# Spatial transforms of a spectral block in four 64x64 parts of the matmul array

## The reference, cut to what matters

```python
# layer 0: whitening over all 50,176 tokens
m = mean(x_flat); f = x_flat - m
ff = (1 - EPS) * (f @ f.T / (n - 1)) + EPS * eye(64)
x = (inv(cholesky(ff)) @ f) * gamma + beta
# layer 1: spectral filter, then MLP
residual = x
h = layer_norm(x, n1_g, n1_b)                      # over the 64 channels
xf = rfft2(h, axes=(height, width), norm='ortho')  # 56 x 29 frequencies
o1 = relu(complex product of xf with w1, 8 blocks of 8 channels, + b1)
o2 = softshrink(complex product of o1 with w2 + b2, 0.01)
h = irfft2(o2) + h + residual
out = gelu(layer_norm(h, n2_g, n2_b) @ mw1 + mb1) @ mw2 + mb2 + h
```

## Time and profile before

| | |
|---|---|
| median of three runs | 841.62 us (840.57 to 844.27) |
| profiled execution, device time | 842.9 us |
| its span, first to last instruction | 841.1 us |
| TensorE busy | 778.3 us, 93% |
| VectorE busy | 569.4 us, 68% |
| ScalarE busy | 378.4 us, 45% |
| GpSimd busy | 251.9 us, 30% |
| mean granted clock of TensorE, share of 2.4 GHz | 0.932 |

### The profile page before, as it was taken

The page is one execution under the profiler, slowest core; times in us unless marked ns, Lnnn a source line. Parts: engine busy times, 40 slices in busy tenths (PEclk is TensorE's granted clock), DMA queues, the critical chain, the costliest instruction groups (busy, mean ns, idle before and its releaser), DMA issues.

```text
span 841.1 us, 17115 instructions
## 1 busy us (share of the span) xinstructions
PE 778.3 (93%) x6823; PEld 542.9 (65%) x6823; DVE 569.4 (68%) x1860; ACT 378.4 (45%) x687; POOL 251.9 (30%) x107
## 2 busy tenths in 40 slices
PE   7999996986799999999999999999999998989987
PEld 5985555875477667666766667676757664746433
DVE  4567777279577767776776777677867695843551
ACT  0011005623164735563556455545554545455455
POOL 4000000932903270427042604360435045413000
PEclk9895557899699999999999999999999999999999
DMA  9943002002000121002100300030001001001012
GB/s 263 276 113 107 1 0 75 3 2 78 1 1 13 34 65 46 24 23 82 29 25 23 95 17 24 23 108 4 23 23 34 2 24 34 23 2 34 23 34 67
DMA packets 10369, 39.41 MB, mean 47 GB/s; under 512 B 1282, under 2 KB 1410, under 8 KB 8834
## 3 DMA queue, kind: packets, MB, share of 16 engines
q1 hardware_dynamic: 10290, 38.31, 15.8%
HBM read 25.46 MB, written 12.85 MB: 46 GB/s over the span
## 4 chain that ended last, share of the span: by engine, by line
PE 80%; DVE 15%; issue 3%; ACT 1%; DMA 0%; DVEq 0%; ACTq 0%
PE psum L1069 11%; PE psum L1078 10%; PE psum L982 7%; PE psum L1047 6%; PE psum L992 6%; PE psum L1023 6%; PE psum L1034 6%; PE psum L1007 6%; PE psum L966 5%; PE psum L829 4%; PE psum L886 4%; DVE stats L588 3%; PE psum L1087 3%; PE psum L953 2%; PE psum L1060 2%
## 5 line engine op out<-in xcount | busy, mean ns | idle before, releaser
L1271 ACT ACTIVATE hid<-psum,hbias 128x448 f32<-128x448 f32 x224 | 124.0, 636 | 80.6 <-PE psum L1069 80.6
L436 POOL TENSOR_TENSOR p_y<-layer,clamped 128x512 f32<-128x512 f32 x64 | 75.5, 1180 | 240.1 <-DVE clamped L698 240.1
L1069 PE MATMUL psum<-n2T,mw1s 64*128 64x448 f32 x448 | 102.7, 577 | 1.7 <-ACT n2T L1264 1.7
L1078 PE MATMUL psum<-hid,prm 128*64 128x448 f32 x448 | 96.3, 552 | 2.0 <-DVE oslice L707 2.0
L401 POOL TENSOR_TENSOR hbuf<-hbuf,prm 112x3584 f32<-112x3584 f32 x7 | 43.4, 6205 | 111.1 <-DVE hbuf L653 111.1
L1047 PE MATMUL psum<-u_r,cst 58*112 58x448 f32 x256 | 60.4, 592 | 15.5 <-DVE rbuf L720 11.3
L1023 PEld LDWEIGHTS psum<-w2s,o_g 128*64 128x64 f32 x1856 | 60.1, 138 | 15.5 <-issue 8.9
L692 DVE TENSOR_TENSOR layer<-psum,prm 128x512 f32<-128x512 f32 x64 | 40.4, 631 | 41.6 <-PE psum L1023 41.6
L1034 PEld LDWEIGHTS psum<-cst,p_y 128*128 128x128 f32 x512 | 61.2, 192 | 11.2 <-issue 5.6
L1023 PE MATMUL psum<-w2s,o_g 128*64 128x64 f32 x1856 | 66.3, 224 | 2.1 <-DVE layer L692 2.1
L1034 PE MATMUL psum<-cst,p_y 128*128 128x112 f32 x512 | 66.7, 277 | 1.2 <-DVE layer L692 1.2
(11 more groups left out here) (130 smaller groups left out, 1308.7 us busy)
## 6 DMA issues: line engine op xcount, KB each, us to landing
xin<-x_dram SPq DMA_DIRECT2D x8, 1568.0 KB, 8.3
out_dram<-oslice SPq DMA_DIRECT2D x56, 224.0 KB, 2.2
ybuf<-x_dram SPq DMA_DIRECT2D x2, 1568.0 KB, 16.8
fbuf<-x_dram SPq DMA_DIRECT2D x2, 1568.0 KB, 19.9
xin<-x_dram SPq DMA_DIRECT2D x4, 392.0 KB, 5.2
n<-x_dram SPq DMA_DIRECT2D x1, 1568.0 KB, 22.1
n<-x_dram SPq DMA_DIRECT2D x4, 392.0 KB, 15.7
prm<-params_dram SPq DMA_DIRECT2D x1, 742.0 KB, 3.9
```

What stands on the lines that cost most here:

```text
L436: nc.gpsimd.tensor_tensor(yk, a, b, ALU.subtract).then_inc(y_ready, 1)
L1069: nc.tensor.matmul(t[:, 0:4 * ROWS], mw1s[C * v:C * v + C, HH * m:HH * m + HH], n2T[C * v:C * v + C, s % 2, :], start=True, stop=True).the ...
L1078: last = nc.tensor.matmul(t[C * v:C * v + C, 0:4 * ROWS], pp("mw2")[:, C * m:C * m + C], hid[:, s % 2, m, v, :], start=(m == 0), stop=(m = ...
L1271: nc.scalar.activation(hid[:, s % 2, m, v, :], bank[CH_MLP[i].bank[k]][:, 0:4 * ROWS], ACT.Gelu, bias=hbias[:, m:m + 1]).then_inc(c_act, 1)
```

## The change

- Tiles whose partitions are rows of images have 128 partitions and not 112: image 0 on 0 to 55, image 1 on 64 to 119 (`RP` is 128); only the loads of x still come with 112. Between them lie rows of zeros, which two more memsets (`mlp_t`, `xT`) and columns of zeros in the constants provide.
- `dft_h` and `dft_w` are cut into matmuls on 64x64 parts of the array. In `dft_h` image b is on the part's rows (partition 64 b) and channel half h on its columns; in `dft_w` the halves are on the rows and the images on the columns. `f1` and `f2` shrink to 58 columns. A chunk now has eight groups of 58 columns; two chunks (two banks) are filled together, and both banks are waited for before the first matmul.
- h lies as (channel j, half h, place w). g1 and b1 then repeat along w.
- ScalarE's copies and activations keep their number, except in step 0, where `dft_w` has one activation for a chunk and not two.
- Whitening, the transpositions and the inverse column transform work on 128 partitions or columns where they had 112.
- Two store DMAs for a slice, one for each image.
- VectorE: `ev_mlp` of pair i-2 comes behind all four `ln2_stats`, and `multiply_rstd` of the second half moves from `ln2` to the end of slice 0 (`second_half`), in front of the first statistics of the next pair.

The core of the diff:

```diff
+RP = 128
-CONST_COLS = {"ident": 128, "below": C, "minus": C, "f1": 2 * KR, "f2": 4 * KF, "invw": 112, "invh": 2 * ROWS,
+CONST_COLS = {"ident": 128, "below": C, "minus": C, "f1": KR, "f2": KR, "invw": 112, "invh": 2 * RP,
...
-        u_v = u_r[0:ROWS, :].rearrange("p (m j) -> p m j", j=CH)
+        u_v = u_r[0:C + H, :].rearrange("p (k b s j) -> p k b s j", b=2, s=2, j=CH)
+        xT_v = xT[:].rearrange("p (w b r) -> p w b r", b=2, r=C)[:, :, :, 0:H]
+        mlp_t_v = mlp_t[:].rearrange("p (w b r) -> p w b r", b=2, r=C)[:, :, :, 0:H]
...
-        h_w = h_nat.rearrange("p (j m) -> p j m", j=CH)
-        h_tok = h_nat.rearrange("p (j w h) -> p w j h", j=CH, h=2)
+        h_w = h_nat.rearrange("p (j h w) -> p j h w", j=CH, h=2)
+        h_tok = h_nat.rearrange("p (j h w) -> p w j h", j=CH, h=2)
...
-                    sp.dma_start(o[:, s * SW * C:(s + 1) * SW * C], oslice[:, s % 2, :]).then_inc(stored[s % 2], 16)
+                    for b in range(2):
+                        sp.dma_start(o[H * b:H * b + H, s * SW * C:(s + 1) * SW * C],
+                                     oslice[C * b:C * b + H, s % 2, :]).then_inc(stored[s % 2], 16)
...
+                nc.gpsimd.memset(mlp_t[:], 0.0).then_inc(s_ones, 1)
+                nc.gpsimd.memset(xT[:], 0.0).then_inc(s_ones, 1)
...
-                    nc.gpsimd.tensor_tensor(h4, h4, g, ALU.mult).then_inc(h_scaled, 1)
+                    nc.gpsimd.tensor_tensor(h3, h3, row_h("g1"), ALU.mult).then_inc(h_scaled, 1)
...
+                    nc.vector.memset(bank[7], 0.0)
...
                 def ln2(i):
                     mean_rstd(i, 1)
                     if i < PAIRS - 2:
                         ev_whiten(i + 2, [0])
-                    for k in range(2):
-                        multiply_rstd(i, k)
+                    multiply_rstd(i, 0)
...
                     if behind:
-                        ln2_stats(i - 1, 4)
+                        for k in range(4, 8):
+                            ln2_stats(i - 1, k)
                         if i > 1:
                             ev_mlp(i - 2, SLICES - 1)
-                        for k in range(5, 8):
-                            ln2_stats(i - 1, k)
                         ln2(i - 1)
+                    def second_half():
+                        if behind:
+                            multiply_rstd(i - 1, 1)
+                        next_(ln1_stats, [0])
...
-                           lambda: next_(ev_whiten, [6]), lambda: next_(ln1_stats, [0]))
+                           lambda: next_(ev_whiten, [6]), second_half)
...
-                            last = nc.tensor.matmul(t[0:ROWS, j * 128:(j + 1) * 128], xT[:, w * ROWS:(w + 1) * ROWS],
+                            last = nc.tensor.matmul(t[:, j * 128:(j + 1) * 128], xT[:, w * RP:(w + 1) * RP],
...
-                    for k in range(8):
+                    for k in range(0, 8, 2):
                         if i > 1 and k == 2:
                             mlp_out(i - 2, SLICES - 1)
                         if i > 1 and k == 4:
                             turn_out(i - 2, SLICES - 1)
-                        t = free_b(i, S1 + k)
-                        for j in range(4):
-                            last = nc.tensor.matmul(t[0:ROWS, j * 2 * KR:(j + 1) * 2 * KR], h_w[:, 4 * k + j, :],
-                                                    cc("f1", ROWS), start=True, stop=True)
-                        last.then_inc(pe_b, 1)
+                        t = [free_b(i, S1 + k + b) for b in range(2)]
+                        for j in range(8):
+                            for b in range(2):
+                                for h in range(2):
+                                    one = nc.tensor.matmul(t[b][C * h:C * h + H, j * KR:(j + 1) * KR],
+                                                           h_w[C * b:C * b + H, 4 * k + j, h, :], cc("f1")[C * b:C * b + H, :],
+                                                           start=True, stop=True)
+                                if j == 7:
+                                    one.then_inc(pe_b, 1)
...
-                    for k in range(8):
-                        t = free_b(i, S2 + k)
-                        for j in range(min(4, KF - 4 * k)):
-                            last = nc.tensor.matmul(t[:, j * 4 * KF:(j + 1) * 4 * KF], u_r[0:ROWS, (4 * k + j) * 128:(4 * k + j + 1) * 128],
-                                                    cc("f2", ROWS), start=True, stop=True)
-                        last.then_inc(pe_b, 1)
+                    for k in range(0, 8, 2):
+                        t = [free_b(i, S2 + k + h) for h in range(2)]
+                        n = min(8, KF - 4 * k)
+                        for j in range(n):
+                            at = (4 * k + j) * 128
+                            for h in range(2):
+                                for b in range(2):
+                                    one = nc.tensor.matmul(t[h][C * b:C * b + C, j * KR:(j + 1) * KR],
+                                                           u_r[C * h:C * h + H, at + C * b:at + C * b + C], cc("f2")[C * h:C * h + H, :],
+                                                           start=True, stop=True)
+                                if j == n - 1:
+                                    one.then_inc(pe_b, 1)
...
-                        nc.scalar.copy(u_v[:, :, 4 * k:4 * k + 4],
-                                       bank[B_BANK[S1 + k]][0:ROWS, 0:8 * KR].rearrange("p (j m) -> p m j", j=4)
-                                       ).then_inc(b_act, 1)
+                        js = slice(8 * (k // 2), 8 * (k // 2) + 8)
+                        nc.scalar.copy(u_v[:, :, k % 2, :, js], bank[B_BANK[S1 + k]][0:C + H, 0:8 * KR].rearrange(
+                            "p (j k s) -> p k s j", j=8, s=2)).then_inc(b_act, 1)
...
+                act.wait_ge(s_ones, MEMSETS + 2)
```

146 lines of the change are left out of this document (67 added, 79 removed).

## The result

The changed kernel takes 889.66 us (median of four runs, 889.45 to 891.81) where the kernel before took 842.94 (four runs beside it, 840.57 to 846.08): a ratio of 1.0567, interval 1.0537 to 1.0597. It is 47 us slower; I had forecast 835 us and a range up to 854.

A forecast was written before the change was run, and what follows sets the result against it. TensorE's own queue was taken as the limit almost everywhere. Steps -16.0, costs +4.8 and clock +4.5 us summed to -6.7: 842.9 to 836.2 profiled, 835 us as median; range for 8 in 10 from 818 to 854.

The forecast's parts named there:

- through `dft_w` at 399.1: Steps 2 to 6: TensorE, at 104 and 118 ns, ends `dft_w` at 399.1 and then waits 4 us.
- The pace of four parts (104 and 118 ns for eight records): Both transforms: four parts run side by side, giving 3.3 us for `dft_h` and 3.4 for `dft_w`.
- Rival (a): TensorE takes at most two parts at once, or feeds records no faster than 29.5 ns: 852 us; chance 0.23.
- h's new layout at nothing for VectorE: No cost entered for VectorE's write of h; VectorE's work on 128 partitions takes the same time as on 112.
- Rival (b): GpSimd slows reading h in single 4-byte words, up to 2.5 ns an element: 846 us; chance 0.10.
- Step 0, -5.2 us: Step 0: faster transforms let layer 1 start at 160.0 and not 165.22.
- Steps 2 to 6, -1.1 us each before costs: Middle steps: VectorE frees bank 0 at 403.0, layer 1 starts at 404.1 for 405.22; five steps, -5.5.
- The 4 us of idle TensorE before whitening chunk 1: Steps 2 to 6: TensorE, done with `dft_w`, waits 4 us until VectorE frees bank 0.
- Costs of the padding, +4.8 us: Costs sum: n2's transpositions +2.9, whitening +1.6, second store DMA +0.3 us.
- The clock, +4.5 us: Steps 2 to 6: the waits lower TensorE's clock, bounds 0 and 1.7 us a step, 0.9 taken.
- rival (d): The clock falls for longer, or twice a step, 1.7 us and more in steps 1 to 6: 841 us; chance 0.08.
- Lies in the wait for the first loads: Kernel start: two new memsets on GpSimd and one on VectorE lie in the wait for the first loads.

The follow-up runs named there:

- e2: Changed kernel with SyncE's load of the next pair held until the step's `dft_w` is issued (steps 1 to 5): 874.91 us, ratio 1.0417.
- e5: Changed kernel with the edits of e1, e2 and e3 together: 840.89 us, ratio 0.9989 to the kernel before.
- e7: Changed kernel with `dft_w` in two parts of 64 by 128 instead of four of 64 by 64: 894.46 us, ratio 1.0621.
- e3: Changed kernel with h laid in memory as before the change (channel, column, half): 874.44 us, ratio 1.0399.
- e1: Changed kernel with VectorE's six products of weights and masks issued ahead of the first pair's LayerNorm statistics: 874.99 us, ratio 1.0403.
- e4: Changed kernel with VectorE's order as before the change: 894.14 us, ratio 1.0623.
- e8: Kernel before with VectorE's new order alone: 841.26 us, ratio 0.9988.
- e9: e5 with four parts in `dft_h` only, `dft_w` again one matmul a channel pair, ScalarE's copies behind it as before: 839.77 us, ratio 0.9969.
- e10: e9 without e2's late load: 837.90 us, ratio 0.9956.

## Why the prediction was wrong, point by point

The step that failed first is the time of the transforms: 3.4 us for `dft_w`, with TensorE "through `dft_w` at 399.1". In step 3 `dft_w` took 10.45 us (424.98 to 435.43), since TensorE waited for instructions.

- **The pace of four parts (104 and 118 ns for eight records): right.** Measured 105 in `dft_h` and, in the undisturbed row of 127 records of e2 and e5, (2.09 - 0.23)/126 x 8 = 118 in `dft_w`. Rival (a) fell, and with it the estimate of about 200 ns from the Trainium skill ("TensorEngine Tiling (Array Packing)", section "Instruction Overhead"): a record every 13.2 ns shows that here that floor was not the engine's.
- **What can stop TensorE between its records: the cause of that failure.** I took the engine's pace from rows with few instructions in a row and asked only for banks, ports and the clock. `dft_h` and `dft_w` are 488 pairs of load and matmul records a step for 122, and instructions come in blocks of 256. I named no supply of instructions at all, and did not read the instruction queue's line on the page. It cost 30.2 + 3.6 us of idle TensorE in sum, 24.3 of it in the four long stalls of steps 2 to 5, and the clock with it (below). The number of instructions and the load both count: e7 halves the one and e2 moves the other, and either takes the long stalls away. The Trainium skill ("Runtime: NRT & Kernel Launch", section "Instruction fetch mechanics") says that blocks of 256 instructions are fetched ahead while the current one runs, and that this is mostly hidden. The trace agrees on the blocks (256 instructions to an access), and not on the hiding: 5.5 to 6.8 us at a time lay bare.
- **h's new layout at nothing for VectorE: the second.** I had looked at the width of VectorE's operations (128 partitions for 112, indeed free) and not at the stride of their output. Writing h in single words 224 bytes apart takes 3521 ns for 2023, e3 takes it back: 14.1 us. Rival (b) had the layout, but on GpSimd's scaling, which stayed at 6.20 us; of GpSimd only the residuals slowed, to 2.7 to 2.8 ns an element, above my bound of 2.5.
- **Step 0, -5.2 us: the third.** The products of weights and masks were in none of my lists: in the kernel before they cost 0.29 us each and nothing waited for them. I had told the rule of the shared port, and used it only where it already bit. e1: 13.8 us. Freed of it and of the layout (e5), step 0 starts 3.2 us later than before and takes 4.2 us less, and from `dft_h` to layer 1 it takes 13.5 us for 16.8: two thirds of what I forecast.
- **Steps 2 to 6, -1.1 us each before costs: borne out in two steps of five, and only in e5.** Layer 1 of step 3 starts 15.2 us behind `dft_h` for 17.0 before; `dft_h` itself starts 0.5 us later for its two banks, which leaves -1.3. Steps 3 and 4 take 0.9 us less in all. But step 2 takes 0.0 less, and steps 5 and 6 take 1.9 us more each, so that steps 2 to 6 of e5 take 415.1 us for 413.1. VectorE's side of the mechanism is there: small operations were held beneath the residual (L623, 4.79 us), and bank 0 is free 14.0 us behind the start of `dft_h` in e5 for 14.4 forecast. The 4 us of idle TensorE before whitening chunk 1 never showed: it waited 1.48 us for VectorE in e2 and 0.33 in e5, since waits for instructions (0.47 and 1.90 us in e5) came first. VectorE's new order made no difference where it was tried (e4, e8), but TensorE did not wait for bank 0 there; beside e5 it was not tried.
- **Costs of the padding, +4.8 us: right within 2 us.** The transpositions of n2 (L1078; L1060 before) are 283 ns long for 267. In step 3 of e5 layer 1, layer 2 and the inverse transforms take 0.9 us more. Of that 0.53 is the wait for two banks before `dft_h` (0.75 us for 0.22), which I had forecast apart as 0.45; 0.37 a step is left, some 3 us in eight steps.
- **The clock, +4.5 us: direction right, size far too small.** I had 0.9 us in each of steps 2 to 6 from the wait for bank 0. Measured: 0.50 for 6.8 us in each of steps 2 to 5, beginning 0.8 to 3.4 us before the end of the long stall. In step 3 the 68 records, the whitening and layer 1 take 10.97 us (433.32 to 444.29); the same three take 8.24 in e5, its wait left out: 2.7 us a step, so some 11 us in four steps for 3.6 forecast (an estimate from one step). The condition of rival (d), a longer fall, came true, by a wait that it did not name. Mean granted clock is 0.906 for 0.932 in the two executions; e9, which has the four parts in `dft_h` and hardly a stall, is at 0.939, so the parts don't lower it by themselves.
- **Ahead of step 0, 0:** it starts 7.7 us late. 4.2 of that is the layout (e3). 3.7 are there before VectorE writes h: the last part of the covariance starts at 60.39 us for 56.66 before. In it TensorE waits 1.6 us for the first xT where it waited 0.2, as ScalarE's function table (1.28 us) is loaded only at 47.73, behind the wait for the memsets, and the covariance group behind that wait takes 5.06 us for 3.49, at a granted clock of 0.67 from 50 to 55.2 us. "Lies in the wait for the first loads" was true of the memsets, not of what was made to wait for them.

## What to carry to other kernels

Splitting a matmul into parts multiplies instructions: count them against the blocks of 256 and their closest spacing (3.3 us at the closest here, 7 to 9 beside a large load), and split only where the count stays below, as in `dft_h` alone; even there the gain was 0.3 to 0.4%. Count what an idle stretch of TensorE does to its clock as well. When a layout is turned for one engine, price the strided write on the engine that writes it. And an edit that delays VectorE by a few us near a long GpSimd operation can turn 0.3 us operations into 8 us ones; a wait for the port depends on who comes first, so look at every short two-operand operation within reach.

## What the runs showed of the hardware

- Four 64x64 parts with 58 moving columns take a record every 13.2 ns; two 64x128 parts with the same columns one every 57 ns, in the same total time as one 112x128 matmul with 116 columns.
- Blocks of 256 instructions came no closer than 3.3 us in the changed kernel, and 7.2 to 8.6 us apart at the four long stalls, with a load of 1568 KB at the same time. At each of these stalls the count of executed instructions stood 449 above 256 times the number of blocks asked for; in the kernel before it never stood over 261. I read this as: what was held on the chip had been used up.
- VectorE's fp32 write with a stride of 56 words takes 1.96 ns an element and partition for 1.13 with pairs of words (3521 and 2023 ns for 1792).
- TensorE's granted clock fell to 0.50 for 6.8 us at each of the four waits of 5.5 to 6.8 us in steps 2 to 5 of the changed kernel; with no wait over 1.6 us there (e9, e10) it did not fall.
